# A decoder layer on one core: the first half opened in another order

## The chip, the cores and the metric

The kernel runs on one core of a Trainium2 chip. The metric is the device time of one execution in microseconds (us), taken as the median of several executions. TensorE (PE in the profile) multiplies, VectorE (DVE) and ScalarE (ACT) work element by element and can read PSUM, GpSimd (POOL) works element by element on SBUF, and SyncE (SP) issues most of the transfers.

## The reference

One layer over 2048 tokens (32 sequences of 64) of width 512, all in float32. `x` is normalised (mean and variance over 512), and 32 heads of a decayed linear attention of width 128 follow. With a block length of 32 the scan over blocks is the same as one causal, decayed product over the 64 tokens of a sequence.

```python
x = x + attention(layernorm(x))            # 32 heads, this case's change is in here
x = x + cross_attention(layernorm(x), ctx) # 64-wide queries, keys and values
x = x + layernorm(x) @ identity.T

# attention(h):
qkv  = silu(h @ qkv_w.T)                   # 512 -> 3 * 32 * 128
out  = decayed causal (q k^T) v            # for each sequence and head
normed = norm_w * out / rms(out)
return (sigmoid(h @ gate_w.T) * normed) @ out_w.T
```

## The kernel before

The tokens are worked on in two halves of 1024. A half has eight token tiles of 128, kept in `attn_acc[:, t]`; tiles `p` and `p + 4` form pair `p` (p = 0 to 3). In each half a loop over `d` = 0 to 7 takes four heads at a time, and in each round there are eight projection calls: VA and VB (values of the first and the second two pairs), QK0, QK1, G01, QK2, QK3, G23.

Each projection is a Winograd form of a 2 x 2 block product with seven products instead of eight (`PRODUCTS`). It needs sums of weight blocks, which GpSimd makes (`mix`, four 128x256 operations for each weight tile, the results S1 to S4), and sums of token blocks, T1, T2, T3 and T4N (`token_sums`, four 128x256 operations for each pair). Full float32 precision comes from two-part operands: ScalarE rounds a tile into `hi` (`cut_va`, `cut_qk0` and so on, `turned_hi`), VectorE subtracts to get `lo` (`cut_a`, `cut_b`, `cut_c`, `turned_lo`), and each product is made of hi·hi, hi·lo and lo·hi. In a value call a product is 12 matmuls of 256 columns, 84 in the call.

Before its products can run, the normalised x must be turned (transposed) by TensorE through PSUM. Each pair has four pieces r = 0 to 3: (B11, B21), (B22, T1), (T2, T3) and (T4N); the first three take 4 transposes each, and the last takes 2. After them comes a `turned_hi` on ScalarE and a `turned_lo` on VectorE.

The order of the work is written out by hand for each engine and is held by semaphores that count upward. At the start of the first half:

- SP loads `ident`, the eight tiles of x (256 KB each), and small tables. ScalarE's queue loads the weights of VA into `raw1` and those of VB into `raw0` (512 KB each).
- GpSimd mixes `raw1`, makes the inverse roots of pair 0 (`inv_roots`), mixes `raw0`, makes the roots of pair 1, then the token sums of pairs 0 to 3.
- ScalarE cuts both weights in two parts (`cut_va`, `cut_vb`), then all eight pieces of pairs 0 and 1.
- VectorE makes the statistics, normalises each pair in place (`normalise`, line 906) and makes the low parts.
- TensorE turns the pieces of pairs 0 and 1 first. In `values` it then waits for `x_ready` 8, `w_a` 2 and `w_b` 2, and turns pairs 2 and 3 inside VA, before products 2, 4 and 6.

The two value calls read both weight tiles. VB starts after `silu_ready` 3, QK0 after `silu_ready` 6 and `w_c` 2 (its weights' low part). In `project` on VectorE the first step is `add_snapshot`, which waits for product 1 of the call; `between` and `last_gap` are places where other work is put in the middle of a call. On ScalarE the matching gaps follow a `snapshot`.

SP waits in the same order each time: for `w_b` 2, and then it loads QK0's weights into `raw0`; for `w_a` 2, and then QK1's weights into `raw1`; for `w_c` 2, and then G01's weights, followed by 2 MB of x for the second half.

Of the kernel before, what the change touches and what calls it, by code (L numbers as in the profile page):

```python
# [17 lines left out]
F32 = mybir.dt.float32  # L18
# [256 lines left out]
def attention(nc, sb, sem, bank, attn_acc, sq_acc, ident, ones, cross, x, w_pairs, w_out, norm_w, decay, ident_in):  # L275


    with ExitStack() as own:
# [5 lines left out]
        def from_column(tensor, first):  # L284
# [20 lines left out]
        wa_hi = weights("w_hi_a", SHIFT)  # L305
        w_hi = [from_column(t, 0) for t in (wa_hi, wb_hi, wc_hi)]
# [28 lines left out]
                                                                            "x_hi_ready", "x_ready"))  # L335
        p_mm, snapped, c_added, c_sig = (sem(n) for n in ("p_mm", "snapped", "c_added", "c_sig"))
# [36 lines left out]

        WITH_VALUES = whole(2)[:3], whole(2)[3:] + whole(3)[:2], whole(3)[2:]

# [9 lines left out]
        def turn_bank(half, p, r):  # L385

            if half == 1 and p >= 2:
                return (0, 1, 7)[(4 * (p - 2) + r) % 3]
            return ((0, 1, 5, 6), (CHAIN, SECOND, THIRD, 7))[half][r]
# [33 lines left out]
        def sync(sp):  # L423
# [68 lines left out]
        def gpsimd(pool):  # L492
# [10 lines left out]

            def token_sums(half, p):

                n = (half * TT + p) * 4
# [105 lines left out]
        def scalar(act):  # L612
# [111 lines left out]
            def turned_hi(half, pieces):  # L724
                for p, r in pieces:
                    act.wait_ge(x_turned, (half * TT + p) * 4 + r + 1)
                    nc.scalar.activation(x_part(x_hi, r, p), turned_part(half, p, r), ACT.Copy).then_inc(x_hi_ready, 1)

# [5 lines left out]
            def body(half, d):  # L734
                previous, following = before(half, d), after(half, d)
                if at(d, 0):
                    project(half, d, VA, *(lambda i=i: turned_hi(half, WITH_VALUES[i]) for i in range(3)))
                    for part in range(2):
                        cut_qk0(half, d, part)
                else:  # L740
                    project(half, d, VA, lambda: cut_qk0(half, d, 0), lambda: cut_qk0(half, d, 1))
                project(half, d, VB)
# [40 lines left out]
            for raw, call, landed in ((raw1, VA, raw1_landed), (raw0, VB, raw0_landed)):  # L783
                act.dma_start(raw[:, 0:4], w_pairs[0, call].rearrange("p (r n) -> p r n", r=4)).then_inc(landed, 16)
            act.wait_ge(consts_set, 2)
            nc.scalar.activation(sigmoid_set[:, :], ones[:, 0:1], ACT.Sigmoid)
            for part in range(2):
                cut_va(0, 0, part)
            for part in range(2):
                cut_vb(0, 0, part)  # L790
            turned_hi(0, whole(0, 1))
# [7 lines left out]
        def vector(dve):  # L799
# [41 lines left out]
            def project(half, d, call, between=None, last_gap=None):  # L841
                add_snapshot(half, d, call, shaped(call, bank[:, SECOND]), result(call, 0, 0), 0)
                silu(half, d, call, 0, 0, SECOND, 1)
# [59 lines left out]
            def normalise(half, p):  # L903
                dve.wait_ge(rstd_ready, p + 1 if half == 0 else TT + 1)
                for t in (p, p + TT):
                    nc.vector.tensor_scalar(attn_acc[:, half * HT + t], attn_acc[:, half * HT + t],
                                            mv[:, t, 0:1], rstd[:, t:t + 1], ALU.subtract,
                                            ALU.mult).then_inc(xn_ready, 1)

            def turned_lo(half, pieces):  # L910
                for p, r in pieces:
                    dve.wait_ge(x_hi_ready, (half * TT + p) * 4 + r + 1)
                    nc.vector.tensor_tensor(x_part(x_lo, r, p), turned_part(half, p, r),
                                            x_part(x_hi, r, p).bitcast(F32), ALU.subtract).then_inc(x_ready, 1)

            def body(half, d):
# [3 lines left out]
                if at(d, 0):  # L920
# [13 lines left out]
                project(half, d, VB)  # L934
# [24 lines left out]
                if before_turning:  # L959
                    normalise(1, 0)  # L960
# [4 lines left out]
                if before_turning:  # L965
                    normalise(1, 1)
# [17 lines left out]
                if before_turning:  # L984
                    normalise(1, 2)
                project_gate(half, d, G23, lambda: cut_out(half, d, 1))
                if before_turning:
                    normalise(1, 3)
# [30 lines left out]

            statistics(0, (0, TT), 0)  # L1020
            statistics(0, (1, 1 + TT), 2)
            normalise(0, 0)
            for part in range(2):
                cut_a(0, 0, 0, part)
            normalise(0, 1)
            statistics(0, (2, 2 + TT), 4)
            for part in range(2):
# [11 lines left out]
        def tensor(pe):  # L1039
# [25 lines left out]
            def project_v(half, d, call):  # L1065

                for n, (a, b, to, part) in enumerate(PRODUCTS):
                    if call == VA and at(d, 0) and n in (2, 4, 6):
# [49 lines left out]
            def turn(half, pieces):  # L1118
                for p, r in pieces:
# [3 lines left out]
                    else:  # L1123
                        pe.wait_ge(t_made, 4 * n + (1, 3, 4)[r - 1])
# [5 lines left out]
                    elif p:  # L1130
                        pe.wait_ge(x_ready, 4 * n - 3 + (r if half == 0 or p < 2 else 3))
# [26 lines left out]
            def values(half, d):  # L1158
                previous = before(half, d)
                turning = half == 1 and at(d, 0)  # L1160
                if at(d, 0):
# [4 lines left out]
                pe.wait_ge(w_a, count(half, d, 6, 2))  # L1166
                pe.wait_ge(w_b, count(half, d, 4, 2))
                project_v(half, d, VA)
                if at(d, 0):
# [82 lines left out]
            turn(0, whole(0, 1))  # L1252
# [333 lines left out]
```

## Time and profile before

| what | value |
|---|---|
| median of 3 runs | 2110.15 us (2109.49 to 2111.38) |
| profiled execution, its own time | 2109.76 us |
| span of the profiled execution | 2107.9 us |
| mean granted TensorE clock | 0.998 of full speed |
| busy share PE / DVE / ACT / POOL | 98% / 66% / 54% / 36% |
| first product of VA, from the span's start | 26.30 us |
| first product of VB | 42.75 us |
| first product of QK0 | 54.41 us |

The span runs from the first to the last recorded instruction; the execution's own time is 1.9 us longer. Times below are counted from the span's start. A matmul's duration in the trace overlaps with the next one's; what it costs in a row is the distance from start to start.

### The profile page before, as it was taken

How to read it: one execution, taken by the hardware profiler on the slowest of the kernel's cores; microseconds unless marked ns; L12 is line 12 of the kernel's file. 1: busy time of each engine (PE TensorE's matmuls, PEld its weight loads, DVE VectorE, ACT ScalarE, POOL GpSimd, SP SyncE). 2: the span in 40 equal slices, each digit the busy share in tenths (PEclk: the TensorE clock that was granted, in tenths of full speed). 3: DMA queues.
4: the chain of work that ended last, by engine and by line, in shares of the span. 5: the costliest groups of instructions: out<-in, count | busy, mean ns of one | idle time of the engine just before them, and what ended most of it. 6: DMA issues, size and time to landing. Idle time of an engine off the chain costs nothing.

```text
span 2107.9 us, 42507 instructions
## 1 busy us (share of the span) xinstructions
PE 2064.4 (98%) x16208; PEld 1694.3 (80%) x16208; DVE 1397.9 (66%) x1992; ACT 1129.4 (54%) x1927; POOL 759.0 (36%) x882
## 2 busy tenths in 40 slices
PE   6999999999999999999999999999999999899998
PEld 5788888888888888888888888888888888666665
DVE  6566666566666666766666666657566666788885
ACT  4545555454545554555554555545455554666664
POOL 6334435252534343543433342525243433111110
PEclk9999999999999999999999999999999999999999
DMA  3121111111112011111111111111111201311110
GB/s 121 54 62 42 62 41 51 51 51 47 55 37 65 30 62 41 46 39 52 52 42 62 41 60 42 51 51 51 41 61 31 71 30 57 131 45 47 46 36 21
DMA packets 40502, 109.49 MB, mean 52 GB/s; under 512 B 4960, under 2 KB 9568, under 8 KB 40288
## 3 DMA queue, kind: packets, MB, share of 16 engines
q1 hardware_dynamic: 40128, 107.25, 16.0%
q8 instruction: 59, 0.97, 0.2%
q10 hardware_dynamic: 288, 1.05, 0.1%
q14 instruction: 27, 0.22, 0.0%
HBM read 104.09 MB, written 4.19 MB: 51 GB/s over the span
## 4 chain that ended last, share of the span: by engine, by line
PE 95%; DVE 3%; ACT 1%; POOL 0%; issue 0%; DMA 0%; SPq 0%; POOLq 0%; DVEq 0%; ACTq 0%
PE bank L1056 15%; PE bank L1061 14%; PE bank L1059 14%; PE bank L1113 6%; PE bank L1114 5%; PE bank L1115 5%; PE bank L1076 5%; PE bank L1081 5%; PE bank L1079 5%; PE bank L1103 4%; PE bank L1091 3%; PE bank L1441 3%; PE bank L1454 3%; PE bank L212 2%; PE bank L1480 1%; PE bank L1463 1%
## 5 line engine op out<-in xcount | busy, mean ns | idle before, releaser
L521 POOL TENSOR_TENSOR raw<-raw 128x256 f32<-128x256 f32 x128 | 126.7, 990 | 598.4 <-DMA raw<-w_pairs 598.4
L1056 PE MATMUL bank<-x_hi,w_hi_c 128*128 128x512 f32 x672 | 266.9, 397 | 2.1 <-DVE v L839 1.5
L1061 PE MATMUL bank<-x_hi,w_lo_c 128*128 128x512 f32 x672 | 262.0, 390 | 0.0
L1059 PE MATMUL bank<-x_lo,w_hi_c 128*128 128x512 f32 x672 | 261.9, 390 | 0.0
L1113 PE MATMUL bank<-wo_hi,y_hi 128*128 128x512 f32 x512 | 202.0, 395 | 3.4 <-DVE y_lo L877 2.4
L1114 PE MATMUL bank<-wo_lo,y_hi 128*128 128x512 f32 x512 | 199.7, 390 | 0.0
L1115 PE MATMUL bank<-wo_hi,y_lo 128*128 128x512 f32 x512 | 199.5, 390 | 0.0
L552 POOL TENSOR_TENSOR sq_acc<-sq_acc,sq 128x512 f32<-128x512 f32 x124 | 161.3, 1300 | 88.9 <-ACT sq L715 79.8
L839 DVE TENSOR_TENSOR qk<-bank,qk 128x512 f32<-128x512 f32 x192 | 127.2, 690 | 85.4 <-ACT qk L686 42.8
L1056 PE MATMUL bank<-x_hi,w_hi_a 128*128 128x512 f32 x448 | 176.0, 393 | 0.0
L1061 PE MATMUL bank<-x_hi,w_lo_a 128*128 128x512 f32 x448 | 174.5, 390 | 0.0
L1059 PE MATMUL bank<-x_lo,w_hi_a 128*128 128x512 f32 x448 | 174.5, 389 | 0.0
L663 ACT ACTIVATE qk<-bank 128x512 f32<-128x512 f32 x192 | 115.6, 602 | 108.0 <-PE bank L1061 107.1
L891 DVE TENSOR_TENSOR attn_acc<-attn_acc,bank 128x512 f32<-128x512 f32 x240 | 163.4, 683 | 14.3 <-PE bank L1115 13.1
L1056 PEld LDWEIGHTS bank<-x_hi,w_hi_c 128*128 128x128 f32 x672 | 126.1, 188 | 34.2 <-ACT qk L663 3.9
L1061 PEld LDWEIGHTS bank<-x_hi,w_lo_c 128*128 128x128 f32 x672 | 126.1, 188 | 26.8
L1059 PEld LDWEIGHTS bank<-x_lo,w_hi_c 128*128 128x128 f32 x672 | 126.2, 188 | 24.8
L832 DVE TENSOR_TENSOR gate<-bank,gate 128x512 f32<-128x512 f32 x96 | 66.4, 692 | 120.0 <-PE bank L1061 120.0
L541 POOL TENSOR_TENSOR qk<-qk,sq 128x512 f32<-128x512 f32 x64 | 82.7, 1292 | 165.7 <-ACT sq L684 165.7
L832 DVE TENSOR_TENSOR bank<-bank,qk 128x512 f32<-128x512 f32 x128 | 89.5, 700 | 78.1 <-PE bank L1061 78.1
L872 DVE TENSOR_TENSOR bank<-bank,gate 128x512 f32<-128x512 f32 x128 | 82.8, 693 | 80.4 <-ACT sq L715 80.4
L722 ACT ACTIVATE y_hi<-bank 128x512 fp32r<-128x512 f32 x128 | 73.1, 599 | 114.0 <-PE bank L1115 103.5
(157 smaller groups left out, 5453.4 us busy)
## 6 DMA issues: line engine op xcount, KB each, us to landing
raw<-w_pairs SPq DMA_DIRECT2D x126, 512.0 KB, 3.6
raw<-w_out SPq DMA_DIRECT2D x32, 512.0 KB, 3.5
xr<-x SPq DMA_DIRECT2D x4, 1024.0 KB, 7.0
raw<-ctx_in SPq DMA_DIRECT2D x16, 256.0 KB, 3.0
raw<-ctx_in SPq DMA_DIRECT2D x32, 128.0 KB, 3.1
out<-attn_acc SPq DMA_DIRECT2D x16, 256.0 KB, 2.0
attn_acc<-x SPq DMA_DIRECT2D x8, 256.0 KB, 6.0
decays<-decay SPq DMA_DIRECT2D x32, 64.0 KB, 3.0
```

Of the source, the lines that this page charges most:

```text
L521: nc.gpsimd.tensor_tensor(raw[:, S1], raw[:, S3], raw[:, A22], ALU.add).then_inc(done, 1)
L552: nc.gpsimd.tensor_tensor(acc, acc, sq[:, b, h], ALU.add).then_inc(sq_added, 1)
L663: nc.scalar.activation(dst, shaped(call, bank[:, (CHAIN, CHAIN, THIRD)[nth]]), ACT.Copy).then_inc(snapped, 1)
L832: nc.vector.tensor_tensor(dst, shaped(call, bank[:, (SECOND, CHAIN, THIRD)[nth]]), src, ALU.add).then_inc(c_added, 1)
L839: nc.vector.tensor_tensor(o, shaped(call, bank[:, at_bank]), o, ALU.mult).then_inc(silu_ready, 1)
L891: nc.vector.tensor_tensor(acc, acc, bank[:, out_bank(i)], ALU.add)\
L1056: nc.tensor.matmul(bank[:, to], w_hi[w][:, a, s], x_hi[:, b, c], start=part in ("first", "only") and c == 0, stop=False, skip_group_check= ...
L1059: nc.tensor.matmul(bank[:, to], w_hi[w][:, a, s], x_lo[:, b, c], start=False, stop=False, skip_group_check=True)
L1061: i = nc.tensor.matmul(bank[:, to], w_lo[w][:, a, s], x_hi[:, b, c], start=False, stop=part in ("last", "only") and c == 1, skip_group_che ...
L1113: nc.tensor.matmul(dst, y_hi[:, h, r], wo_hi[:, h], start=(h == 0), stop=False)
L1114: nc.tensor.matmul(dst, y_hi[:, h, r], wo_lo[:, h], start=False, stop=False)
L1115: k = nc.tensor.matmul(dst, y_lo[:, h, r], wo_hi[:, h], start=False, stop=(h == HG - 1))
```

## The change

The change touches only the opening of the first half, up to the end of VB of the first round.

- Loads: SP issues pair 0 of x first, then `ident`, pair 1, VB's weights (`raw0`), pairs 2 and 3. ScalarE's queue issues only VA's weights.
- GpSimd makes the inverse roots of pairs 0 and 1 first, and a shift, -mean·rstd, in two more small operations for each pair (`shifts`). Then it mixes both weights, makes roots and shifts of pairs 2 and 3, and the token sums of pairs 2 and 3 only.
- Normalising moves from VectorE to ScalarE (`normalise` is now an activation with scale and bias). The token sums of pairs 0 and 1 move from GpSimd to VectorE (`token_sums` there).
- The weights of VA and VB are cut in other portions: blocks 0 and 1 first (before any mixing), blocks 2 to 6 later (`cut_first`).
- TensorE turns only the pieces (0,0) and (1,0) ahead of VA. `values` waits for `x_ready` 2, `w_a` 1 and `w_b` 1; the fuller counts stand before product 2. The other 14 pieces are turned inside VA (before products 2, 4, 6) and VB (before products 1, 2, 4). ScalarE and VectorE get their parts of these pieces, and the cut of QK0's weights, inside the gaps of the two calls.

The hunks stand in this order: SP, the plan of the pieces, GpSimd, ScalarE's opening and its two calls, VectorE's opening and its two calls.

```diff
-            sp.dma_start(ident[:, :], ident_in).then_inc(const_landed, 16)
-            for p in range(TT):
+            def load_tiles(p):
                 for t in (p, p + TT):
                     sp.dma_start(attn_acc[:, t], x_t[t]).then_inc(x_tile_landed[t], 16)
+            load_tiles(0)
+            sp.dma_start(ident[:, :], ident_in).then_inc(const_landed, 16)
+            load_tiles(1)
+            load(raw0, w_pairs[0, VB], raw0_landed)
+            load_tiles(2)
+            load_tiles(3)
...
+        FIRST_ORDER = pieces(0, 0, 2, 1, 3) + pieces(2, 0, 2, 1, 3)
+        FIRST_TURNS = {VA: {2: pieces(0, 2, 1), 4: pieces(0, 3), 6: pieces(2, 0)},
+                       VB: {1: pieces(2, 2), 2: pieces(2, 1), 4: pieces(2, 3)}}
+        FIRST_NEEDS = {VA: {2: 4, 3: 6, 6: 8}, VB: {0: 10, 2: 12, 3: 14, 6: 16}}
+        FIRST_PARTS = slice(0, 2), slice(2, 7)
...
+            for p in range(2):
+                inv_roots(slice(p, HT, TT), 2 * p + 2, p + 1)
+                shifts(p)
             mix1(0, 0, 0, 1)
-            inv_roots(slice(0, HT, TT), 2, 1)
             mix0(0, 0, 0)
-            inv_roots(slice(1, HT, TT), 4, 2)
-            token_sums(0, 0)
-            token_sums(0, 1)
-            inv_roots(slice(2, HT, TT), 6, 3)
+            for p in range(2, TT):
+                inv_roots(slice(p, HT, TT), 2 * p + 2, p + 1)
+                shifts(p)
             token_sums(0, 2)
-            inv_roots(slice(3, HT, TT), 8, 4)
             token_sums(0, 3)
...
+            act.wait_ge(raw1_landed, 16)
+            cut_first(v_hi[0], raw1, 0, hi_a)
+            normalise(0)
+            act.wait_ge(raw0_landed, 16)
+            cut_first(v_hi[1], raw0, 0, hi_b)
+            normalise(1)
+            turned_hi(0, pieces(0, 0))
+            act.wait_ge(mixed1, 4)
+            cut_first(v_hi[0], raw1, 1, hi_a)
+            act.wait_ge(mixed0, 4)
+            cut_first(v_hi[1], raw0, 1, hi_b)
...
+                if half == 0 and at(d, 0):
+                    project(half, d, VA, turned_hi_and_normed, lambda: turned_hi(0, pieces(0, 3)),
+                            lambda: turned_hi(0, pieces(2, 0)))
+                    project(half, d, VB, lambda: turned_hi_and_cut(pieces(2, 2, 1), 0),
+                            lambda: turned_hi_and_cut(pieces(2, 3), 1))
...
             statistics(0, (0, TT), 0)
             statistics(0, (1, 1 + TT), 2)
-            normalise(0, 0)
-            for part in range(2):
-                cut_a(0, 0, 0, part)
-            normalise(0, 1)
+            dve.wait_ge(hi_a, 1)
+            cut_first(v_lo[0], v_hi[0], raw1, 0, w_a)
+            dve.wait_ge(hi_b, 1)
+            cut_first(v_lo[1], v_hi[1], raw0, 0, w_b)
+            token_sums(0)
+            turned_lo(0, pieces(0, 0))
+            token_sums(1)
             statistics(0, (2, 2 + TT), 4)
-            for part in range(2):
-                cut_b(0, 0, 0, part)
-            turned_lo(0, whole(0, 1))
-            normalise(0, 2)
             statistics(0, (3, 3 + TT), 6)
-            normalise(0, 3)
+            dve.wait_ge(hi_a, 2)
+            cut_first(v_lo[0], v_hi[0], raw1, 1, w_a)
+            dve.wait_ge(hi_b, 2)
+            cut_first(v_lo[1], v_hi[1], raw0, 1, w_b)
...
+                if half == 0 and at(d, 0):
+                    project(half, d, VA, lambda: turned_lo(0, pieces(0, 3)), lambda: turned_lo(0, pieces(2, 0)),
+                            lambda: turned_lo(0, pieces(0, 2, 1)))
...
+                    project(half, d, VB, lambda: turned_lo_and_cut(pieces(2, 3)), lambda: cut_c(0, 0, 0, 1),
+                            lambda: turned_lo(0, pieces(2, 2, 1)))
```

`turned_hi_and_normed` is, for p = 2 and 3, `normalise(p)` and then the high parts of pieces (0,2), (1,2) for p = 2 and (0,1), (1,1) for p = 3. The third function of VectorE's `project` is its new first gap, right after the call's first `add_snapshot`.

## Rows read from the trace of the kernel before

**Rows 1.** The page's head: span, and busy time of each engine.
```profile
span 2107.9 us, 42507 instructions
...
PE 2064.4 (98%) x16208; PEld 1694.3 (80%) x16208; DVE 1397.9 (66%) x1992; ACT 1129.4 (54%) x1927; POOL 759.0 (36%) x882
```

**Rows 2.** Waits of PE, 0 to 130 us: waiter, releaser, us in total, times, longest.
```profile
PE bank L1135 <- DVE attn_acc L906: 11.4, 1, 11.4
PE bank L1135 <- POOL sq_acc L512: 3.5, 1, 3.5
...
PE bank L1076 <- DVE v L839: 1.7, 1, 1.7
```

**Rows 3.** The chain that ended last, 0 to 110 us: start, us, what.
```profile
6.70 1.39 DVE stats L898 x2
...
8.72 0.72 POOL rstd L501
...
26.30 0.58 PE bank L1076
...
42.75 0.36 PE bank L1076
...
54.41 0.47 PE bank L1056
```

**Rows 4.** DMA issues, 0 to 60 us: KB each, median us from issue to landing.
```profile
attn_acc<-x SPq DMA_DIRECT2D x8, 256.0 KB, 6.0
...
raw<-w_pairs SPq DMA_DIRECT2D x3, 512.0 KB, 3.6
```

**Rows 5.** Windows: busy time of each engine, clock, DMA share, GB/s, 4 to 5 us.
```profile
4.00:5.00 1.00, 0.00 (x0) 0.00 (x0) 0.00 (x0) 0.00 (x0) 0.12 (x1) 1.00 1.03 404
```

**Rows 6.** Timeline of PE, 0 to 90 us: start, us, line, operation, out<-in, count.
```profile
23.07 1.91 PE L1135 MATMUL bank<-ident,spare 128*128 128x128 f32 x8
...
26.89 0.41 PE L1081 MATMUL bank<-w_hi_a,x_lo 128*128 128x256 f32 x1
27.11 0.41 PE L1076 MATMUL bank<-w_hi_b,x_hi 128*128 128x256 f32 x1
...
29.41 0.28 PE L1081 MATMUL bank<-w_hi_a,x_lo 128*128 128x256 f32 x1
29.53 0.28 PE L1076 MATMUL bank<-w_hi_b,x_hi 128*128 128x256 f32 x1
...
38.82 0.82 PE L1135 MATMUL bank<-ident,qk 128*128 128x128 f32 x6
```

**Rows 7.** Groups by line and shape, ACT, whole span: busy us, mean ns, idle before.
```profile
L727 ACT ACTIVATE x_hi<-bank 128x512 fp32r<-128x512 f32 x24 | 13.6, 603 | 9.4 <-PE bank L1135 9.4
L137 ACT ACTIVATE xn<-attn_acc,shift,rstd 128x512 f32<-128x512 f32 x16 | 13.1, 819 | 5.2 <-POOL shift L115 5.2
```

**Rows 8.** Groups by line and shape, DVE, whole span.
```profile
L802 DVE TENSOR_TENSOR w_lo_c<-raw,w_hi_c 128x1024 fp32r<-128x1024 f32 x48 | 60.5, 1260 | 3.6 <-ACT w_hi_c L615 3.4
...
L913 DVE TENSOR_TENSOR x_lo<-bank,x_hi 128x512 fp32r<-128x512 f32 x24 | 15.4, 684 | 1.1 <-ACT x_hi L727 1.1
```

**Rows 9.** Groups by line and shape, POOL, whole span.
```profile
L524 POOL TENSOR_TENSOR raw<-raw 128x256 f32<-128x256 f32 x128 | 94.9, 742 | 0.0
...
L115 POOL TENSOR_SCALAR shift<-mv,rstd 128x1 f32<-128x1 f32 x32 | 9.0, 282 | 3.3
```

**Rows 10.** Timeline of DVE, 0 to 90 us.
```profile
11.21 3.14 DVE L802 TENSOR_TENSOR w_lo_a<-raw,w_hi_a 128x1024 fp32r<-128x1024 f32 x2
...
66.36 2.09 DVE L802 TENSOR_TENSOR w_lo_b<-raw,w_hi_b 128x1024 fp32r<-128x1024 f32 x2
```

**Rows 11.** Timeline of POOL, 0 to 90 us.
```profile
8.39 0.24 POOL L499 TENSOR_SCALAR rstd<-mv 128x2 f32<-128x2 f32 x1 [0.62 <-DVE mv L901]
...
11.83 1.70 POOL L526 TENSOR_TENSOR raw<-raw 128x256 f32<-128x256 f32 x1
13.51 0.94 POOL L499 TENSOR_SCALAR rstd<-mv 128x2 f32<-128x2 f32 x1
```

More of the change, by code:

```diff
@@ L372, in whole, with pieces, place, sums_made @@
             return tuple((p, r) for p in tiles for r in range(4))
+        def pieces(first, *parts):
+            return tuple((p, r) for r in parts for p in (first, first + 1))
+        FIRST_ORDER = pieces(0, 0, 2, 1, 3) + pieces(2, 0, 2, 1, 3)
[3 more added lines that the diff above has]
+        FIRST_PARTS = slice(0, 2), slice(2, 7)
         WITH_VALUES = whole(2)[:3], whole(2)[3:] + whole(3)[:2], whole(3)[2:]
+        def place(half, p, r):
+            return 16 + 4 * p + r if half else FIRST_ORDER.index((p, r))
+        def sums_made(half, p, r):
+            return 4 * (TT * half + p - 2) + (1, 3, 4)[r - 1] if half or p >= 2 else 4 * p + (1, 3, 4)[r - 1]
         def x_part(tensor, r, p):
@@ L722, in y_high, with turned_hi, normalise, turned_hi_and_cut @@
                     nc.scalar.activation(by_tokens(y_hi, top), y_part(b, top), ACT.Copy).then_inc(y_hi_ready, 1)
-            def turned_hi(half, pieces):
-                for p, r in pieces:
-                    act.wait_ge(x_turned, (half * TT + p) * 4 + r + 1)
+            def turned_hi(half, turned):
+                for p, r in turned:
+                    act.wait_ge(x_turned, place(half, p, r) + 1)
                     nc.scalar.activation(x_part(x_hi, r, p), turned_part(half, p, r), ACT.Copy).then_inc(x_hi_ready, 1)
+            def normalise(p):
+                act.wait_ge(shift_ready, 2 * p + 2)
+                for t in (p, p + TT):
+                    nc.scalar.activation(attn_acc[:, t], attn_acc[:, t], ACT.Identity, bias=shift[:, t:t + 1],
+                                         scale=rstd[:, t:t + 1]).then_inc(xn_ready, 1)
+            def turned_hi_and_cut(turned, part):
+                turned_hi(0, turned)
+                cut_qk0(0, 0, part)
+            def turned_hi_and_normed():
+                for p in (2, 3):
+                    normalise(p)
+                    turned_hi(0, pieces(0, (2, 1)[p - 2]))
             def weighted(half, d, s):
@@ L1067, in project_v @@
                 for n, (a, b, to, part) in enumerate(PRODUCTS):
-                    if call == VA and at(d, 0) and n in (2, 4, 6):
+                    if half == 0 and at(d, 0):
+                        if n in FIRST_TURNS[call]:
+                            turn(half, FIRST_TURNS[call][n])
+                        if n in FIRST_NEEDS[call]:
+                            pe.wait_ge(x_ready, FIRST_NEEDS[call][n])
+                        if call == VA and n == 2:
+                            pe.wait_ge(w_a, 2)
+                            pe.wait_ge(w_b, 2)
+                    elif call == VA and at(d, 0) and n in (2, 4, 6):
                         turn(half, WITH_VALUES[n // 2 - 1])
@@ L1116, in project_out, with turn @@
                 k.then_inc(out_mm, 1)
-            def turn(half, pieces):
-                for p, r in pieces:
+            def turn(half, turned):
+                for p, r in turned:
                     n = half * TT + p
@@ L1129, in turn @@
                         pe.wait_ge(out_added, count(0, LAST, 16, 9 + order))
-                    elif p:
-                        pe.wait_ge(x_ready, 4 * n - 3 + (r if half == 0 or p < 2 else 3))
+                    elif half and p:
+                        pe.wait_ge(x_ready, 4 * n - 3 + (r if p < 2 else 3))
+                    elif half == 0 and place(0, p, r) >= 4:
+                        pe.wait_ge(x_ready, place(0, p, r) - 3)
                     for j, block in enumerate(piece(half, p, r)):
@@ L1160, in values @@
                 turning = half == 1 and at(d, 0)
-                if at(d, 0):
+                if half == 0 and at(d, 0):
+                    pe.wait_ge(x_ready, 2)
+                elif at(d, 0):
                     pe.wait_ge(x_ready, 16 * half + 8)
@@ L1165, in values @@
                     pe.wait_ge(c_sig, count(half, d, 32, 0))
-                pe.wait_ge(w_a, count(half, d, 6, 2))
-                pe.wait_ge(w_b, count(half, d, 4, 2))
+                first = half == 0 and at(d, 0)
+                pe.wait_ge(w_a, count(half, d, 6, 1 if first else 2))
+                pe.wait_ge(w_b, count(half, d, 4, 1 if first else 2))
                 project_v(half, d, VA)
-                if at(d, 0):
+                if at(d, 0) and not first:
                     pe.wait_ge(x_ready, 16 * half + 16)
@@ L1251, in tensor @@
             pe.wait_ge(const_landed, 16)
-            turn(0, whole(0, 1))
+            turn(0, pieces(0, 0))
             for half in range(2):
```

74 lines of the change are left out of this document (49 added, 25 removed).

## The prediction

> **What bounds the kernel now.** I read the page's head first. TensorE is busy for 2064.4 us of 2107.9 [rows 1], so an opening that gets more work out of the other engines is worth only the TensorE idle time that it removes, 43.5 us at most over the whole span. The list of who waits for whom shows where much of it lies: one wait of 11.4 us before the first turning, then 3.5 us for GpSimd's token sums [rows 2]. Both are ahead of 26.30 us, where VA's first product starts.
>
> The chain that ended last says what carries that opening. It begins with x's statistics at 6.70 us, goes through GpSimd's root at 8.72, and reaches VA's first product at 26.30, VB's at 42.75 and QK0's at 54.41 [rows 3]. From QK0 on nothing is edited. So the whole change is worth 54.41 minus the time at which QK0 starts afterwards, if the loads behind it move along. I follow that one instant.
>
> Two rates of TensorE matter. Inside VA two 256-column matmuls start 0.22 us apart at 26.89 and 0.12 us apart at 29.41 [rows 6]. That is the clock's 1.2 GHz and then its 2.4 GHz level, though the window view prints 1.00 for the early stretch too [rows 5]. The engine had to run for 3.1 us (26.30 to 29.41) before the fast spacing came. At the fast one a product of 12 costs 1.41 us; six transposes and their refill take from 38.82 to about 39.4, so 0.1 us each [rows 6].
>
> **The change part by part.**
>
> *Loads.* Now tile 0 of x stands behind `ident` and beside two weight loads: about 1.37 MB have moved when it lands at 6.70 [rows 3]. Afterwards tiles 0 and 4 share with one weight load, 1.05 MB in all. At 404 GB/s [rows 5] tile 4 is there about 0.8 us earlier, at 5.9, and tile 0, with half of that still to come, near 5.1. The bounds are 4.6 and 6.7 (no gain at all). VB's weights, issued fifth, land near 8.4: behind 1.1 MB of x and `ident` on SP's queue, against 6.0 us from issue to landing for a tile of x now [rows 4].
>
> *Roots and shifts.* From the first statistics to the end of the root is 2.74 us now (6.70 to 8.72 plus 0.72) [rows 3]; so 7.85. Two shifts at 0.28 [rows 9] make 8.45. Pair 1 follows at 10.1, and only then does GpSimd start to mix; now it starts with the mixing and has both weights mixed at 13.53 [rows 11].
>
> *Normalising on ScalarE.* The same form with scale and bias takes 0.82 us [rows 7]: pair 0 from 8.45 to 10.0, VB's first weight portion (0.6, as a 512-wide activation [rows 7]) to 10.6, pair 1 to 12.1. Turning piece (1,0) costs 1.1 and its high part 0.6: 13.85.
>
> *VectorE up to the first product.* At 10.6 it cuts VB's first portion, makes four token sums, and two low parts. By itself: 0.6, then 4 x 0.35 + 0.2 (a 1024-wide difference takes 1.26, so 256 wide about 0.35 [rows 8]), then 0.65 twice [rows 8], the last one behind ScalarE's 13.85: `x_ready` 2 at 14.5. But GpSimd mixes from 10.1 on, and all five differences have two inputs in SBUF. What the two do to each other shows at 11.21: two cuts that take 2.09 us when GpSimd is idle took 3.14 [rows 10]. GpSimd's operation that began at 11.83 took 1.70 in place of 0.74, and the root's 128x2 step at 13.51, worth 0.24, took 0.94 [rows 9, 11]. The ends fit one engine waiting for the other: the first ends when the other's does, and the next begins there. Taken so, each of VectorE's differences stands behind a remaining mix operation of 0.6 us: three of the five are full waits and the rest partial, 1.9 us in all. I take `x_ready` 2 at 16.4, and the first product at 16.45, 9.85 us ahead of 26.30.
>
> The Trainium skill, SBUF — State Buffer, section Who interferes with whom, says that a VectorE instruction with two SBUF inputs and a GpSimd instruction that reads SBUF take one shared interface, and that the second one blocks until the first is done. This trace agrees (1.70 us in place of 0.74 [rows 9, 11]). By plain slowing down in the ratio 3.14 to 2.09 the same stretch would come 1.1 us earlier, at 15.3.
>
> *VectorE up to product 2.* This is the step that decides. Behind `x_ready` 2 VectorE has in its queue, before it can take the call's first snapshot: four sums of pair 1 (2.05 with the rest of the mixing), statistics of pairs 2 and 3 (2 x 1.45: 1.39 [rows 3] and the aggregation), and both second weight portions, 1280 wide: 1.4 each from 1.26 for 1024 [rows 8]. Then 0.3 for GpSimd's small steps. 16.4 + 2.05 + 2.9 + 2.8 + 0.3 = 24.45. The first snapshot's add (0.65) and two low parts (1.3) follow: `x_ready` 4 at 26.4. GpSimd's roots and shifts of pair 2, held by the cuts, let ScalarE normalise it at 22.8; with 1.55 and two high parts, 1.15, it is ready at 25.5 and just hidden. Products 0 and 1 and the 16 transposes end near 22.4, so TensorE stands for about 4 us and product 2 starts at 26.5. If VectorE paid nothing to GpSimd, this would be 23.9; that is the lower bound.
>
> *The rest of VA.* The stop of 4 us is near the 3.5 us one [rows 2], after which the slow spacing was still in force, so I let the clock fall and need 3.1 us again: 14 matmuls at 0.215 and 10 at 0.118, products 2 and 3 end at 30.75. Pair 3's high parts, at 28.35, and low parts, at 29.0, come in time for product 3. Four transposes 0.5, products 4 and 5 2.8, eight transposes 0.85, product 6 1.4: 36.35. The silu at the end of the call gives VB 1.6 us later (VB's wait for the silu is 1.7 now [rows 2]): 38.0.
>
> *VB.* Now 42.75 to 54.41, 11.66 us [rows 3]. Added: 20 transposes, 2.1. Product 2 waits for low parts queued behind the snapshot's add, which waits for product 1: 2.0 minus the 0.85 of turning, 1.2. Product 6 waits for the add behind the first part of QK0's cut (two half pieces 0.8, cut 1.25, add 0.65, against 2.8 of products): 0.5. The cut's second part before the last silu: 0.3. So 15.75, and QK0 starts at 53.8. VA gives back what VB's longer course takes: of 9.85 us won at the first product, 0.6 is left.
>
> *Behind it.* QK0's weights are asked for at 24.5 (21.0 now), land 3.6 later [rows 4], and are mixed after the sums of pairs 2 and 3, 5.8 us of GpSimd at 0.73 each [rows 9]: about 34.5. The cut is due at 41, so 6 us of cover stand there; if it were gone, each further microsecond would be QK0's. G01's weights are asked for at about 53 instead of 45, land at 57, and are mixed at 60 and cut after QK0's last activation, near 64: still hidden. Everything later moves with TensorE.
>
> **The sum.** 54.41 - 53.8 = 0.6 us. The profiled execution took 2109.76 us of its own, 0.4 under the median; by its own time the result is 2109.2, and 2109.5 on the median's.
>
> **The rivals.**
>
> 1. *The shared interface costs less on short operations* than on the cuts at 11.21. For it: only long differences are seen here, and VectorE may slip in between two of GpSimd's. Against: the 0.94 for a step of 0.24 [rows 11] is a short one. Product 2 would start between 23.9 and 24.9, QK0 near 51.7: 2.7 us gained, 2107.4. Chance 0.20.
> 2. *The clock stays up across the stop before product 2.* In this opening nothing stops TensorE for more than 1.7 us once it is fast [rows 2]. The 14 slow matmuls save 0.1 each, 1.4 us: 2108.1, chance 0.10. Together with rival 1, where the stop shrinks to 2 or 3 us and the clock has more reason to hold, it is 4.1 us or a little more: 2106.0 or under, chance 0.12.
> 3. *Slower: the clock stays low through the broken-up calls.* Eight transposes at 23.07 kept TensorE busy for 1.91 us, and yet the products from 26.30 ran at the slow spacing [rows 6]. VA and VB are now cut up by turning and waits. If the remaining 46 matmuls of VA and 12 of VB also ran slow, that is 58 x 0.097 = 5.6 us: 2115.1. It turns the sign at 6 such matmuls and decides at 50. Against it: 3.1 us of products brought the clock up at 29.41, and from product 4 on there is more than that in a row. Chance 0.06. The Trainium skill, TensorE: Matmul & The Clock Gate, section Part 4: PE-mode transpose, says that transposes don't count as busy for the clock in the way matmuls do; the slow spacing at 26.89 after the turning at 23.07 [rows 6] goes with it, though a wait lies between them.
>
> My forecast has 0.50, and 0.02 is for what I don't see. A change within 0.2% (4.2 us) is about what a measurement of this kernel can't tell from none. Over 4.2 us faster are two thirds of the joined case and tails of rivals 1 and 2: 0.14. Slower are rival 3 and a tail of the forecast, should product 2 come 4 us later than summed: 0.09. The rest, 0.77, is the same. The range takes in rivals 1 and 2 and most of both together on one side, and on the other a VectorE queue 2.5 us longer: 2105.5 to 2112.0. The likeliest case's own is 2107.9 to 2111.3.
>
> **What would show it.** Right: first product near 16.4 and product 2 near 26.5, released by a low part; a stop of about 4 us between them, slow spacing after it; GpSimd's mixing stretched to 1 us and more an operation; two short stops in VB; QK0 near 53.8. Wrong: x's first tile later than 6 us; product 2 before 25 us; QK0 under 50.2 (faster) or over 58.6 (slower); a new wait for G01's weights.

## The result, and the profile after

The changed kernel took 2113.76 us (median of 20 runs, 2111.28 to 2119.09) against 2110.14 for the kernel before (20 runs): a ratio of 1.0016, 95% interval 1.0010 to 1.0022. It is slower by 3.6 us. That is under the 0.2% that I called "the same", but it is clear of no change, and it lies above my range, which ended at 2112.0. The profiled execution took 2114.95 us.

The page's head of the changed kernel, for [rows 1]:

```profile
span 2113.1 us, 42520 instructions
...
PE 2067.4 (98%) x16208; PEld 1696.8 (80%) x16208; DVE 1395.9 (66%) x1992; ACT 1132.6 (54%) x1935; POOL 754.6 (36%) x882
```

TensorE has the same 16208 matmuls and is busy for 3.0 us longer. Work was not added, so part of it ran at a lower clock. Its waits in the first 130 us, for [rows 2]:

```profile
PE bank L1237 <- ACT attn_acc L763: 12.4, 2, 11.6
PE bank L1176 <- DVE x_lo L988: 8.8, 3, 4.6
...
PE bank L1148 <- DVE v L900: 1.8, 1, 1.8
```

The wait before the first turning is as long as it was (11.6 and 11.4). The 3.5 us for GpSimd's sums are gone. Low parts of x, for which TensorE waited 2.5 us before a turning and 1.3 us before VA's first product, now cost 8.8 us: 3.0 before the first product, 4.6 before product 2, 1.1 in VB. The chain that ended last, for [rows 3]:

```profile
6.69 0.70 DVE stats L961
7.77 0.25 POOL rstd L524
8.09 0.74 POOL rstd L526
8.93 1.02 POOL shift_x L532 x2
9.97 1.52 ACT attn_acc L763 x2
...
16.37 1.20 DVE x_lo L988 x2
...
22.22 3.08 POOL shift_x L532 x2
25.33 1.52 ACT attn_acc L763 x2
26.85 0.49 ACT x_hi L758
27.36 1.30 DVE x_lo L988 x2
28.70 0.58 PE bank L1176
...
41.80 0.39 PE bank L1176
...
57.91 0.47 PE bank L1148
```

The first product starts at 17.62, 8.7 us ahead of 26.30. Product 2 starts at 28.70, VB at 41.80 (0.95 ahead of 42.75), and QK0 at 57.91, 3.5 us behind 54.41. One window view shows what the clock did (the column before the DMA share is the granted clock):

```profile
24.00:28.70 4.70, 0.08 (x1) 0.00 (x0) 3.06 (x4) 3.37 (x6) 4.43 (x8) 0.93 0.52 176
28.70:34.40 5.70, 5.70 (x26) 5.70 (x27) 1.89 (x3) 2.73 (x6) 5.46 (x9) 0.50 0.11 42
58.00:59.00 1.00, 1.00 (x4) 0.79 (x5) 0.00 (x0) 0.00 (x0) 0.00 (x0) 0.89 0.80 131
59.00:62.00 3.00, 3.00 (x8) 2.32 (x7) 0.00 (x0) 1.55 (x2) 0.97 (x2) 0.50 1.00 336
```

Products 2 and 3 ran at 0.50, which is the 1.2 GHz level, after TensorE had stood for 4.6 us. The fall itself came inside that stop, near 28.1 us. The same happened to QK0 from about 59 to 62 us. The first scores (q times k, made from QK0's result) then begin at 70.71 against 65.64, 5.07 us late, and the span ends 5.2 us late: nothing behind gives it back.

### The profile page after: what moved, and what is told of

Its sections match the earlier page's. It is cut to its first block, busy times and chain, and to the rows that moved or that the text cites. A ratio compares the mean times of both kernels' runs of the same rounds, so it can differ in the third digit from the quotient of the medians.

```text
span 2113.1 us, 42520 instructions
## 1 busy us (share of the span) xinstructions
PE 2067.4 (98%) x16208; PEld 1696.8 (80%) x16208; DVE 1395.9 (66%) x1992; ACT 1132.6 (54%) x1935; POOL 754.6 (36%) x882
## 4 chain that ended last, share of the span: by engine, by line
PE 94%; DVE 3%; ACT 1%; POOL 0%; issue 0%; DMA 0%; SPq 0%; POOLq 0%; DVEq 0%; ACTq 0%
PE bank L1148 15%; PE bank L1153 14%; PE bank L1151 14%; PE bank L1213 6%; PE bank L1214 5%; PE bank L1215 5%; PE bank L1176 5%; PE bank L1181 5%; PE bank L1179 5%; PE bank L1203 4%; PE bank L1191 3%; PE bank L1546 3%; PE bank L1559 3%; PE bank L212 2%; PE bank L1585 1%; PE bank L1568 1%
## 5 line engine op out<-in xcount | busy, mean ns | idle before, releaser
L954 DVE TENSOR_TENSOR attn_acc<-attn_acc,bank 128x512 f32<-128x512 f32 x240 | 162.8, 681 | 14.3 <-PE bank L1215 13.1
L1153 PEld LDWEIGHTS bank<-x_hi,w_lo_c 128*128 128x128 f32 x672 | 126.6, 188 | 27.1
L1176 PE MATMUL bank<-w_hi_a,x_hi 128*128 128x256 f32 x448 | 129.3, 289 | 11.6 <-DVE x_lo L988 9.5
```

What stands on the lines that cost most here:

```text
L954: nc.vector.tensor_tensor(acc, acc, bank[:, out_bank(i)], ALU.add)\
L1153: i = nc.tensor.matmul(bank[:, to], w_lo[w][:, a, s], x_hi[:, b, c], start=False, stop=part in ("last", "only") and c == 1, skip_group_che ...
L1176: nc.tensor.matmul(dst, x_hi[:, b, c, s], v_hi[c][:, a], start=part in ("first", "only") and c == 0 and j == 0, stop=False, skip_group_che ...
```

## The experiments

There are twelve runs. The table puts them side by side: the start of VA's first product, of VA's product 2, of VB and of QK0, and the time from QK0 to the first scores (11.2 us at the full clock). All times are in us.

| kernel | first | prod. 2 | VB | QK0 | to scores | median | ratio, 95% interval |
|---|---|---|---|---|---|---|---|
| before | 26.30 | | 42.75 | 54.41 | 11.2 | 2110.1 | 1 |
| changed | 17.62 | 28.70 | 41.80 | 57.91 | 12.8 | 2113.8 | 1.0016 (1.0010 to 1.0022) |
| changed, again | 17.51 | 28.59 | 40.79 | 56.89 | 11.2 | 2112.5 | 1.0011 (1.0002 to 1.0021) |
| e1 statistics early | 17.61 | 25.62 | 37.28 | 53.38 | 11.2 | 2110.4 | 0.9998 (0.9989 to 1.0007) |
| e3 shift first | 17.40 | 27.29 | 38.95 | 55.06 | 11.2 | 2112.5 | 1.0003 (0.9994 to 1.0012) |
| e2 one stop filled | 17.34 | 28.43 | 39.66 | 55.79 | 12.8 | 2111.9 | 1.0006 (0.9997 to 1.0015) |
| e5 all stops filled | 17.30 | 28.39 | 39.67 | 55.74 | 11.2 | 2111.0 | 1.0004 (0.9995 to 1.0013) |
| e7 mixing late | 16.12 | 31.03 | 43.34 | 59.44 | 11.2 | 2114.9 | 1.0018 (1.0009 to 1.0028) |
| e8 normalised on DVE | 18.39 | 28.92 | 42.91 | 58.98 | 11.2 | 2113.5 | 1.0015 (1.0006 to 1.0025) |
| e4 loads only | 27.04 | | 43.48 | 55.14 | 11.2 | 2111.4 | 1.0003 (0.9994 to 1.0012) |
| e6 e1 + VB's turns early | 17.38 | 25.38 | 37.05 | 50.89 | 11.2 | 2107.6 | 0.9988 (0.9978 to 0.9997) |
| e11 e6 again | 16.91 | 24.91 | 36.56 | 50.39 | 12.8 | 2107.2 | 0.9988 (0.9979 to 0.9997) |
| e10 VB's turns alone | 17.58 | 28.67 | 40.85 | 54.67 | 11.2 | 2112.0 | 1.0010 (1.0001 to 1.0019) |
| e9 e6, two small moves | 17.61 | 25.62 | 37.26 | 51.11 | 12.8 | 2108.5 | 0.9994 (0.9985 to 1.0003) |

Each ratio is taken against the kernel before as measured together with that run (2110.3, 2110.3, 2109.2 and 2109.9 us for the four sets of the experiments). By the intervals the changed kernel (both times), e7, e8 and e10 are slower than the kernel before, e6 and e11 are faster, and the others can't be told from it. Every kernel's times spread over 4 to 9 us. In the traces the stretch from the first scores to the span's end, which no edit touches, takes 2040.0 to 2047.9 us; the clock falls there near 1756 and 1842 us in some traces and after 2097 us in all. So the milestones of the opening show what an edit does there, and the medians show whether it is worth anything in the end.

**The changed kernel again.**

> The changed kernel once more, unedited. If the loss is the schedule's own, QK0 starts within 0.5 us of 57.91 again. If the fall of the clock early in QK0 (matmuls 0.43 us apart between 59.0 and 62.2) is a fixed consequence of the stops in VB, it is there again and QK1 starts 5.1 us later than in the kernel before; if it depends on something that differs from run to run, it is gone or elsewhere, and QK1 is 3.5 us late.

QK0 started at 56.89, 1.02 us from 57.91 where I had expected at most 0.5. The fall in QK0 was not there, and the first scores are 2.5 us late, not 3.5:

```profile
28.60:31.00 2.40, 2.11 (x13) 1.82 (x13) 1.38 (x3) 2.25 (x5) 2.32 (x4) 0.72 0.23 92
31.00:34.00 3.00, 3.00 (x18) 3.00 (x19) 0.51 (x1) 0.70 (x2) 2.84 (x5) 0.66 0.03 5
56.90:60.00 3.10, 3.10 (x14) 2.54 (x15) 0.06 (x1) 1.44 (x2) 0.17 (x1) 1.00 0.78 228
```

These are windows of the second trace of the same kernel. The schedule repeats (28.59 against 28.70); the clock's fall does not. Here it came late in product 2 and ended at 33.1 instead of 34.9. From product 2 to VB it took 12.20 us against 13.10; e1 and e3 below need 11.66 with the clock up, so the fall cost 0.5 us here and 1.4 us in the first trace. Of the 2.5 us by which QK0 is late here, about 1.9 are then the schedule's own. The whole execution was slow all the same, 2117.8 us: its stretch behind the first scores is 5.5 us longer than in the first trace, and the clock fell in it at 1760 and at 1845 us, where the first trace has no fall.

**Who sets product 2: e1, e3.** The edits; the moved statistics are e1, the wait for `shift_ready` is e3:

```diff
             cut_first(v_lo[0], v_hi[0], raw1, 0, w_a)
+            statistics(0, (2, 2 + TT), 4)
             dve.wait_ge(hi_b, 1)
...
             token_sums(1)
-            statistics(0, (2, 2 + TT), 4)
             statistics(0, (3, 3 + TT), 6)
+            dve.wait_ge(shift_ready, 6)
             dve.wait_ge(hi_a, 2)
```

> The changed kernel with the statistics of pair 2 moved into VectorE's idle time before VB's first weight portion. Theory 1 (GpSimd's shift of pair 2 stands behind VectorE's two long differences, 3.07 us for what takes 0.5, and ScalarE's normalising behind it): the shift of pair 2 is made near 20 us, ScalarE normalises pair 2 by 21.5, and product 2 of VA starts at 26 to 26.5, where VectorE's own queue allows it, in place of 28.70: QK0 2.2 to 2.7 us earlier. Rival (VectorE's queue alone sets product 2): the move shortens that queue by 1.4 us, so 27.3. By both the first product keeps within 0.3 us of 17.62.

> The changed kernel with one wait more: VectorE starts the two 1280-wide differences only when GpSimd's shifts of pair 2 are made. Theory 1: VectorE loses 0.4 us, but ScalarE normalises pair 2 from 22.8 in place of 25.33; product 2 then hangs on VectorE's queue and starts near 27.4, 1.3 us earlier. Rival (VectorE's queue alone): product 2 starts 0.4 us later, 29.1.

The changed kernel first: GpSimd's two shifts of pair 2, and VectorE's two cuts, from its timelines.

```profile
22.22 1.59 POOL L532 TENSOR_SCALAR shift_x<-mv,rstd 128x1 f32<-128x1 f32 x1
...
23.79 1.51 POOL L532 TENSOR_SCALAR shift_x<-mv,rstd 128x1 f32<-128x1 f32 x1
```

```profile
22.30 1.46 DVE L1107 TENSOR_TENSOR w_lo_a<-raw,w_hi_a 128x1280 fp32r<-128x1280 f32 x1
23.68 1.48 DVE L1107 TENSOR_TENSOR w_lo_b<-raw,w_hi_b 128x1280 fp32r<-128x1280 f32 x1
```

A shift of one column, 0.26 us by itself, lasts as long as the cut beside it, once for each. Now e3, the timelines of the same two engines:

```profile
22.00 0.50 POOL L532 TENSOR_SCALAR shift_x<-mv,rstd 128x1 f32<-128x1 f32 x2
```

```profile
22.54 1.49 DVE L1107 TENSOR_TENSOR w_lo_a<-raw,w_hi_a 128x1280 fp32r<-128x1280 f32 x1 [0.37 <-POOL shift_x L532]
```

With one more wait VectorE lost 0.37 us and product 2 came 1.4 us earlier, at 27.29 (27.4 expected; the rival said 29.1); 0.2 of it is x landing earlier in that execution, as the first product shows. Both shifts together took 0.50. In e1 the shifts were made at 19.79, ScalarE normalised pair 2 at 21.14, and product 2 started at 25.62, 3.1 us earlier and 0.4 under what I expected; the rival had 27.3. The whole of that went to QK0, and 1.4 us more, because the stop shrank to 1.69 us and the clock stayed up. Theory 1 holds: product 2 waited for the shift, not for VectorE's queue. e3 decides it alone, since it makes VectorE's queue longer and product 2 still comes earlier.

The order in ScalarE's queue makes this wait. Product 2 needs the high parts of pieces (0,2) and (1,2), which belong to pairs 0 and 1 and are turned from 22.17 us on. ScalarE makes them only behind `normalise(2)`, and that waits for pair 2's shifts. To make these high parts first is the obvious other cure; no run tried it.

With the clock up a second wait shows behind product 2: in e1 and e3 TensorE stood for 1.05 us before product 3, for pair 3's low parts (ready at 28.3 and 29.95). In the first trace of the changed kernel they were ready at 31.0, and the slow product 2 lasted until 31.4, so the low clock hid this wait.

**The clock: e2, e5.** The stops are filled with matmuls whose result nobody reads:

```diff
+            def filler(times):
+                for _ in range(times):
+                    nc.tensor.matmul(bank[:, 7, 0:2 * P], x_hi[:, 0, 0, 0:P], v_hi[0][:, 0], start=True, stop=True)
...
+                        if call == VA and n == 2:
+                            filler(36)
```

e5 has `filler(8)` before product 2 of VB and `filler(13)` after each value call besides.

> The changed kernel with 36 matmuls of 256 columns into an unused PSUM bank in TensorE's stop before product 2 of VA (23.9 to 28.7 us); their result is never read. Theory 2 (the stop lets the clock fall to 1.2 GHz, and products 2 and 3 run at it): granted clock 1.0 throughout VA, the two products take 2.8 us instead of 5.3, VB and QK0 start 2.5 us earlier, and the time falls by about 2.5 us. Rival (the slow spacing comes with the operands or with the engines' contention, not with the stop): no change, or later by what the extra matmuls overrun.

> The changed kernel with matmuls into an unused bank in all four stops: 36 before product 2 of VA, 13 after VA, 8 before product 2 of VB, 13 after VB. In the run with the first stop alone filled the clock still fell, at 56 to 60 us, in QK0. If the stops of VA's end and of VB cause that fall, it is gone here: QK0 near 55.8 with 0.23 us between its matmuls from the start, QK1's scores at 67.0 in place of 68.6. If the fall belongs to something in QK0 itself, it is there again.

Windows of e2:

```profile
24.00:31.00 7.00, 6.32 (x53) 6.06 (x51) 4.33 (x7) 5.84 (x10) 6.66 (x12) 1.00 0.47 152
...
55.80:58.00 2.20, 2.20 (x6) 1.76 (x7) 0.00 (x0) 0.00 (x0) 0.00 (x0) 0.61 0.83 240
58.00:60.00 2.00, 2.00 (x7) 1.52 (x6) 0.00 (x0) 1.54 (x2) 0.93 (x2) 0.58 0.98 322
```

and of e5:

```profile
24.00:55.70 31.70, 29.96 (x246) 28.76 (x244) 18.21 (x29) 18.16 (x33) 16.29 (x23) 1.00 0.10 35
55.80:60.00 4.20, 4.20 (x19) 3.46 (x20) 0.70 (x1) 2.04 (x3) 1.24 (x2) 1.00 0.94 283
```

In e2 the clock stayed at 1.00 through VA, and VB started at 39.66: 2.1 us ahead of the first trace of the changed kernel and 1.1 ahead of the second, where I had expected 2.5. In QK0 it fell all the same, and the median (2111.9 against 2112.5 for the changed kernel beside it) doesn't show the gain. In e5 it did not fall anywhere in the opening, and the scores came at 66.95, as expected. The fall in QK0 is in four of the eleven traces that have the changed opening and VB's stops unfilled (the changed kernel, e2, e9, e11: the four with 12.8 in the table), and costs 1.6 us each time. The other seven don't have it either way, so the one trace of e5 doesn't show that the filling prevents it, and what brings this fall on stays open. That the fall in VA follows the long stop is shown by e1, e3 and e2 together. In all five traces in which TensorE stood 3.3 us or longer before product 2 the clock fell by that product's end, and in the five with 0.7 to 2.3 us it didn't. The Trainium skill, TensorE: Matmul & The Clock Gate, section Part 1: The HAM clock gate, puts both levels and the fall after idling down to such a gate, and says that the point of change varies with where in its cycle the work begins. The two traces of the changed kernel agree: the clock was low from about 28.1 us in one, and from 29.6 us, late in product 2, in the other.

**What VB costs: e6, e10, e11.** The edit (e10 alone, e6 and e11 on top of e1):

```diff
-                       VB: {1: pieces(2, 2), 2: pieces(2, 1), 4: pieces(2, 3)}}
+                       VB: {1: pieces(2, 1), 4: pieces(2, 3)}}
...
+                if first:
+                    turn(0, pieces(2, 2))
                 pe.wait_ge(silu_ready, count(half, d, 18, 3))
...
+                    turned_hi(0, pieces(2, 2))
+                    project(half, d, VB, lambda: turned_hi_and_cut(pieces(2, 1), 0),
...
+                    turned_lo(0, pieces(2, 2, 1))
+                    project(half, d, VB, lambda: turned_lo_and_cut(pieces(2, 3)), lambda: cut_c(0, 0, 0, 1))
```

> The run with pair 2's statistics early (QK0 at 53.38), and in VB two things earlier: pieces (2,2) and (3,2) are turned ahead of VB's wait for the silu, and VectorE makes the low parts of (2,2), (3,2), (2,1), (3,1) before the call's first add. Theory 3 (VB is 4.4 us longer than before because 20 transposes and two waits of low parts lie on TensorE's path, in a call that had none): VB's course from its first product to QK0's falls from 16.1 to 14.0 to 14.3 us, and QK0 starts at 51.2 to 51.6, about 3 us ahead of the kernel before; time 2107.5. Rival (VB's length comes from the final chain with the cut of QK0's weights in it): 15.7 or more, QK0 at 53.

> The changed kernel with VB's turns early alone, pair 2's statistics left where the change has them. Theory 3 (VB's length is its own, whatever comes ahead): VB's course to QK0 is 13.8 to 13.9 us in place of 16.1, while VB starts at 40.8 to 41.8 as in the changed kernel; QK0 at 54.6 to 55.7, about equal to the kernel before or 1 us late; ratio 1.000 to 1.0008. If the two moves only work together, VB's course stays near 16.

> The fastest version so far once more (pair 2's statistics early and VB's turns early), to see whether its lead over the kernel before holds. By the trace it starts QK0 3.5 us ahead of the kernel before, so the ratio should be 0.9983 to 0.9990 when the clock's falls elsewhere are shared alike. If the earlier 0.9988 was luck, 0.9995 or more.

From VB's first product to QK0 the changed kernel takes 16.11 us (57.91 - 41.80), and the same within 0.04 in six other runs. With the edit it is 13.84 in e6 (50.89 - 37.05), 13.82 in e10 and 13.83 in e11. The chain of waits of e6 has no low part of x before a product of VB any more, up to this end:

```profile
49.26 0.89 DVE w_lo_c L864
50.14 0.61 DVE v L901
...
50.89 0.47 PE bank L1149
```

So 2.3 of VB's 4.4 extra us were eight transposes on TensorE's path and the wait for their low parts (1.1), while TensorE stood for 1.6 us just before them. What the earlier turning and the earlier low parts give each by itself was not measured. The remaining 2.2 are, by the rows, twelve transposes (about 1.3), 0.3 to 0.5 before product 6, and 0.3 before QK0: the cut of QK0's weights ahead of the last silu takes VectorE 0.89 us (above), but TensorE's last stop is only 1.80 us long where it was 1.50. Rival and theory had 15.7 and 14.0 to 14.3.

e10 started QK0 at 54.67, as expected, 0.26 us behind the kernel before. Its ratio, 1.0010, is a little over the 1.000 to 1.0008 that I expected, and 2 us in the median for 0.26 in the trace stay unexplained. With both moves the kernel is faster than before in two separate sets, 0.9988 each (expected for the second: 0.9983 to 0.9990). This opening's idea pays once its two new waits are gone.

**Single parts: e4, e7, e8.**

> The kernel before with nothing but the new order of the loads (x's first pair ahead of ident and of VB's weights). The first statistics start at 5.8 in place of 6.70, but VA's weights land 1.1 later and VB's at 9.4, and GpSimd mixes VA's weights ahead of the first root: root at 9.9 in place of 9.4, and QK0 0.2 to 0.8 us later than 54.41. Time the same within what is measured.

The first statistics started at 5.84. The root ended at 10.17 (9.9 expected, 9.44 in the kernel before), and QK0 started at 55.14, 0.7 us late. By itself the new order of loads costs this in the trace, because GpSimd mixes VA's weights before anything else and these land 1.3 us later; the timing can't tell the two kernels apart.

> The changed kernel, but GpSimd starts to mix the weights only when VectorE has made all eight token sums of pairs 0 and 1. Theory 1b (a mix operation and a VectorE difference with two SBUF inputs exclude each other, and this cost the sums of pair 0 about 2 us): the four sums at 12.8 take 1.6 us in place of 3.6, the first product starts near 15.6 in place of 17.6, while the mixing comes out at 0.73 an operation and ends near 23. Product 2 then waits for the second weight portions, 27 to 29 us. Rival (the sums are slow for a reason of their own, such as waiting for one another): the sums still take over 3 us and the first product starts at 17.6.

The edit is `pool.wait_ge(first_t_made, 8)` ahead of `mix1(0, 0, 0, 1)`. The sums of pair 0 on VectorE's timeline, first the changed kernel, then e7:

```profile
12.82 0.94 DVE L971 TENSOR_TENSOR sq_acc<-attn_acc 128x256 f32<-128x256 f32 x1
13.69 0.94 DVE L972 TENSOR_TENSOR sq_acc<-attn_acc 128x256 f32<-128x256 f32 x1
```

```profile
12.77 0.42 DVE L972 TENSOR_TENSOR sq_acc<-attn_acc 128x256 f32<-128x256 f32 x1
13.11 0.42 DVE L973 TENSOR_TENSOR sq_acc<-attn_acc 128x256 f32<-128x256 f32 x1
```

A sum starts every 0.87 us beside the mixing and every 0.34 without. The first product came at 16.12, where I had 15.6: by then ScalarE's high part, not the sums, was last. The mixing ended at 24.7, where I had 23, and one of its operations took 1.97 us beside VectorE's cut. That put product 2 at 31.03, past the 27 to 29 that I expected, and made this kernel the slowest, 2114.9 us.

> The changed kernel with the normalising of pairs 0 and 1 back on VectorE (0.54 us a tile, no shift on GpSimd), pairs 2 and 3 still on ScalarE. If the move to ScalarE with its shifts costs at the start, turning begins at 10.1 in place of 11.6 and the first product at 16.6 to 17.0 in place of 17.6. Product 2 is set by the shifts of pair 2 behind the two cuts all the same, so it comes only as much earlier as the first product, near 27.9, and the time stays above the kernel before by 1 to 3 us. If the opening's first step set the end, QK0 would move by the full 1.5.

Turning began at 9.66, 2.0 us earlier (0.4 of it is x landing earlier in that execution), and still the first product came at 18.39, 0.8 us later, where I had expected it up to 1 us earlier. VectorE's timeline says why:

```profile
8.54 0.97 DVE L985 TENSOR_SCALAR attn_acc<-attn_acc,mv,rstd 128x512 f32<-128x512 f32 x2
...
10.73 1.80 DVE L985 TENSOR_SCALAR attn_acc<-attn_acc,mv,rstd 128x512 f32<-128x512 f32 x2 [0.62 <-POOL rstd L526]
12.46 1.21 DVE L1110 TENSOR_TENSOR w_lo_b<-raw,w_hi_b 128x512 fp32r<-128x512 f32 x1
```

Pair 0 was normalised in 0.97 us beside GpSimd's small steps, pair 1 in 1.80 beside the mixing. The move to ScalarE is therefore no cost of the change; it keeps that work off the contested path. Product 2 came at 28.92, not near 27.9, and the median is 3.2 us above the kernel before.

**Two small moves: e9.** VectorE waits for `shift_ready` 2 before its first low part, and ScalarE cuts VB's first portion before it normalises pair 0.

> The run with VB's turns early (QK0 at 50.89), and two small moves in the opening: VectorE makes the low part of VA's first weight portion only when GpSimd's shifts of pair 0 are made (they took 1.01 us for 0.5 behind it), and ScalarE cuts VB's first portion ahead of normalising pair 0. Theory 1 once more at another place: ScalarE starts to normalise at 9.5 to 9.6 in place of 9.95, pair 1 is normalised 0.8 us earlier, the first product starts at 16.7 to 17.0 and QK0 0.4 to 0.6 us earlier, near 50.4. Rival: the first product waits for the sums between GpSimd's mixing, which also starts as before, so nothing moves. The time is 2107 to 2107.5 by the first, 2107.6 by the second: too close for the timing, the trace decides.

The shifts of pair 0 took 0.51 us in place of 1.01, but GpSimd's next step was held instead, and from GpSimd's mixing on all was as before: first product at 17.61 (the rival's answer), QK0 at 51.11. ScalarE began to normalise at 10.04, not at 9.5 to 9.6: VB's weights landed only at 9.50, and their cut now stood ahead. The first product hangs on the sums between the mixing operations, not on what normalises pair 0. The median, 2108.5, is 0.9 us over that of e6, which the intervals don't separate.

## Why the prediction was wrong

I forecast QK0 at 53.8 and it came at 57.91. The shape was right: 8 to 10 us won at the first product, and nearly all of it given back before QK0. The sizes were not, and nearly all erred on the same side.

- **The loads.** Tile 0 and tile 4 landed at 5.81 and 6.69; I had 5.1 and 5.9. I let the bytes ahead of them decide at one rate. The first product was 1.2 us later than summed (17.62 against 16.45), some 0.7 of it from here: it moved with x's landing in e3 and e11 too.
- **The exclusion of VectorE and GpSimd.** Each waits for the other's current operation, as I took it, and e7 shows it (0.87 against 0.34 us a sum). The cut and the four sums lost 2.2 us to it (4.25 us against 2.08 in e7), where I had 1.9. One slip went the other way: I put the 1.9 on top of 14.5, a time set by ScalarE; VectorE's own queue with it ends at 16.0 (10.6 + 0.6 + 1.6 + 1.9 + 1.3). Rival 1 is refuted.
- **The step that failed** is "GpSimd's roots and shifts of pair 2, held by the cuts, let ScalarE normalise it at 22.8". I let both shifts pass behind one cut. They are two operations, each stood behind a cut of its own (1.59 and 1.51 us), and ScalarE started at 25.33. Of these 2.5 us one cut is 1.5; the rest came down from the statistics, which ended 1.1 us later than in my sum. VectorE's queue itself was 0.65 us later than I had it (25.1 against 24.45 at the cuts' end), so that product 2 could have come at 27.1; it came at 28.70. The sentence "just hidden" was the error: I had the right rule and counted the operations on the other side wrongly. e3 and e1 show it.
- **The clock in VA.** That it would fall was right. I priced the low level at 3.1 us; all 24 matmuls of products 2 and 3 and the turning behind them ran at it in the first trace (0.50 from 28.70 to 34.40), and less than that in the second. With the low level's length and the transposes at it, product 2 to VB took 13.1 us where I had 11.5, and 12.2 in the second trace. But "come in time for product 3" was wrong as well: with the clock up TensorE waits 1.05 us there (e1, e3), and product 2 to VB takes 11.66. Against that the low clock cost 1.4 us in the first trace, just what I had. This was luck: it lasted for 24 matmuls instead of 14, and hid the wait that I had left out.
- **VB.** 16.11 against 15.75 summed: right but for 0.35. The wait before product 2 was 1.10 us (1.2 summed), that before product 6 0.30 (0.5), and the last stop 0.30 longer (0.3).
- **The clock in QK0.** Not foreseen at all: 1.6 us in four traces of eleven. My rival 3 had the clock stay low from VA into VB; what happened is a fall after VB's short stops.
- **Behind it.** G01's weights, asked for late, cost nothing that shows: TensorE's list of waits up to 130 us has none for them and has the same 2.9 us for the scores as before, and from the first scores to the span's end the two kernels take 2042.4 and 2042.3 us.

Sum: 2.2 at product 2, 1.6 from there to VB, 0.35 in VB is 4.1 us, and 1.6 in QK0. Against the 0.6 us that I expected to gain this gives QK0 3.5 late and the scores 5.1 late in the profiled execution. In the second trace the scores are 2.5 late (68.11 against 65.64). The mean of the two, 3.8, is near the 3.6 us of the medians, but two traces are few, and the second set of timings has only 2.2 us between its medians. The range's upper end took a queue 2.5 us longer and nothing more for the clock. Either trace's lateness is over it: the delay at product 2 alone (2.2 us) nearly used it up.

## What to carry to other kernels

Starting TensorE earlier is worth nothing by itself; follow the instant at which the old and the new order meet again, and look for what the work moved into the middle must still wait for. When two engines exclude each other, count operations, not time: a tiny step loses as much as the long one beside it, once for each tiny step, so make such steps before the long ones are queued or join them into one. Put turning where TensorE stands anyway: here eight transposes moved by one wait, with their low parts ahead of a blocked add, gave 2.3 us. And look at what stands ahead of a needed step in its own engine's queue: here high parts of pairs 0 and 1 stood behind the normalising of pair 2.

## What the runs showed of the hardware

- VectorE's normalising, one tile in and two per-partition scalars, is held by GpSimd too: 1.80 us for two tiles beside the mixing, 0.97 without (e8).
- GpSimd and VectorE hold each other operation by operation: a shift of one column took 1.59 and 1.51 us beside VectorE's two cuts (1.46 and 1.48 us) and 0.26 by itself; a mixing operation of 0.73 us took 1.97 beside such a cut (e7).
- Before VA's product 2 or in it the granted clock fell after stops of 3.33, 3.87, 3.89, 4.62 and 7.49 us (e8, the changed kernel again, e10, the changed kernel, e7). It did not fall after stops of 0.71 to 2.34 us (e6, e9, e11, e1, e3). In QK0 it fell in four traces, in which TensorE had not stood for longer than 1.8 us at a time since VA's product 3, and not in seven others with the same 1.8 us stop ahead of QK0.
- The clock's changes differ between executions of one kernel, at much the same places of the schedule: VA's product 2, the start of QK0, near 1756 and 1842 us, and the last 11 us. The cost could be read for two of them: 0.5 and 1.4 us in VA, 1.6 us in QK0, as much as the edits studied here.
- The column of the granted clock prints 1.00 from the first product of VA on, while its matmuls start 0.21 us apart until 21.2 us and 0.12 apart behind that. Ahead of the first fall in a trace the spacing of the matmuls has to be read instead.
